# Attention logits of a graph network: one folded query weight, queries and keys on both partition halves, 64-row blocks that alternate between the halves

## The reference, cut to what matters

```python
h = jnp.maximum(_layernorm(x, axis=-1), 0.0)
x = x + _L1_gnn_ref(h, adj, W1, W2, W3, U1, U2, ln_g, ln_b)

# in _L1_gnn_ref
def _top_p_attention(X, W1, W2, W3):
    q = X @ W1.T @ W2.T            # W1 64 x 128, W2 64 x 64
    k = X @ W3.T                   # W3 64 x 128
    logits = q @ k.T / TAU         # 2048 x 2048, contraction 64
    probs = jax.nn.softmax(logits, axis=-1)
    idx = jnp.argsort(-probs, axis=-1)
    sp = jnp.take_along_axis(probs, idx, axis=-1)
    cs = jnp.cumsum(sp, axis=-1)
    keep_sorted = cs - sp < TOP_P
    ...
    A = probs * mask
    return A / jnp.maximum(A.sum(-1, keepdims=True), 1e-12)
for n in range(STEPS):             # 2
    A = _top_p_attention(Xa, W1, W2, W3)
    Xf = R @ Xf                    # R: adj + eye, rows normed
    Xa = A @ Xa
    Z = Z + Xf @ U1[n].T + Xa @ U2[n].T
```

## Time and profile before

| | us |
|---|---|
| median of 3 runs (lowest, highest) | 1067.96 (1066.7, 1069.11) |
| span of the profiled execution, first to last instruction | 1063.4 |
| TensorE busy, VectorE busy, ScalarE busy | 838.8, 779.5, 510.0 |
| mean granted clock of TensorE | 0.899 of 2.4 GHz |

### The profile page before, as it was taken

The page is one execution under the profiler, slowest core; times in us unless marked ns, Lnnn a source line. Parts: engine busy times, 40 slices in busy tenths (PEclk is TensorE's granted clock), DMA queues, the critical chain, the costliest instruction groups (busy, mean ns, idle before and its releaser), DMA issues.

```text
span 1063.4 us, 12286 instructions
## 1 busy us (share of the span) xinstructions
PE 838.8 (79%) x3886; PEld 566.1 (53%) x3886; DVE 779.5 (73%) x2363; ACT 510.0 (48%) x979; POOL 69.7 (7%) x68
## 2 busy tenths in 40 slices
PE   5889958887887853939779878868658999996695
PEld 4844425655665642737256557547447475553342
DVE  5968779888987998971697899889789702326715
ACT  4877235357368376413552664674775232023212
POOL 0020110000000000000000000010001100002201
PEclk9899998998988995969799789989789999998798
DMA  9849304424004000000043320230260456500001
GB/s 339 344 174 431 119 8 151 132 106 159 1 1 159 1 0 2 1 2 1 1 158 124 108 88 1 79 136 1 59 269 15 153 238 253 221 1 0 1 0 40
DMA packets 20221, 108.25 MB, mean 102 GB/s; under 512 B 1824, under 2 KB 8752, under 8 KB 9776
## 3 DMA queue, kind: packets, MB, share of 16 engines
q1 hardware_dynamic: 18752, 106.77, 27.0%
q10 hardware_dynamic: 1392, 0.61, 0.2%
HBM read 88.23 MB, written 19.14 MB: 101 GB/s over the span
## 4 chain that ended last, share of the span: by engine, by line
PE 46%; DVE 27%; ACT 13%; issue 9%; POOL 2%; DMA 1%; DVEq 1%; POOLq 0%; SPq 0%; ACTq 0%
PE PS L808 10%; DVE AT L1520 8%; PE PS L743 6%; PE PS L676 5%; PE PS L546 5%; DVE mxv L1659 4%; PE PS L877 3%; ACT BC L1249 3%; ACT AT L1249 3%; DVE nd L1523 3%; PE PS L1060 3%; PE PS L1036 3%; PE PS L1066 2%; DVE AT L2106 2%; ACT AT L1082 2%
## 5 line engine op out<-in xcount | busy, mean ns | idle before, releaser
L1082 ACT ACTIVATE AT<-PS 128x512 f32<-128x512 f32 (+2 forms) x240 | 118.8, 561 | 121.3 <-PE PS L546 103.7
L743 PE MATMUL PS<-K,ST 128*128 128x512 f32 x224 | 125.6, 713 | 13.0 <-ACT EA L1217 7.6
L546 PE MATMUL PS<-ident,AT 128*128 128x128 f32 x544 | 85.5, 293 | 55.4 <-DVE rS L2161 24.5
L1520 DVE SCALAR_TENSOR_TENSOR AT<-EA,se 128x2048 uint8<-128x2048 f32 (+1 forms) x46 | 107.6, 2345 | 1.6 <-DVE se L1513 0.3
L546 PEld LDWEIGHTS PS<-ident,AT 128*128 128x128 f32 x544 | 68.7, 152 | 64.0 <-DVE rS L2161 26.1
L1520 DVE SCALAR_TENSOR_TENSOR AT<-AT 128x2048 uint8<-128x2048 f32 (+2 forms) x48 | 96.1, 2002 | 2.0 <-PE PS L546 1.1
L1659 DVE TENSOR_REDUCE mxv<-PS 128x1 f32<-128x2048 f32 x32 | 73.3, 2289 | 26.0 <-PE PS L743 20.4
L743 PEld LDWEIGHTS PS<-K,ST 128*128 128x128 f32 x224 | 49.4, 232 | 73.1 <-issue 73.0
L2106 DVE MAX8 AT<-AT 128x8 f32<-128x256 f32 x256 | 87.6, 412 | 0.7
L808 PE MATMUL PS<-hr,AT 128*128 128x128 f32 x512 | 69.8, 285 | 9.2 <-ACT AT L1082 8.4
L808 PE MATMUL PS<-AT 128*128 128x128 f32 x512 | 68.3, 281 | 8.7 <-ACT AT L1082 8.1
(11 more groups left out here) (297 smaller groups left out, 1473.1 us busy)
## 6 DMA issues: line engine op xcount, KB each, us to landing
AT<-keep_at SPq DMA_DIRECT2D x32, 1024.0 KB, 5.1
EA<-in_adj SPq DMA_DIRECT2D x20, 1024.0 KB, 6.8
keep_at<-AT SPq DMA_DIRECT2D x8, 2048.0 KB, 24.9
AT<-keep_at SPq DMA_DIRECT2D x8, 2048.0 KB, 12.3
AT<-in_adj SPq DMA_DIRECT2D x12, 1024.0 KB, 5.0
EA<-keep_degrees SPq DMA_DIRECT2D x1, 1024.0 KB, 6.5
keep_x<-K SPq DMA_DIRECT2D x4, 256.0 KB, 8.6
out<-EA SPq DMA_DIRECT2D x4, 256.0 KB, 2.3
```

The costliest lines, as they stand in the source:

```text
L546: return pe.transpose(dst, src, ident[0:p, 0:p])
L743: mm = pe.matmul(bank(half(gi, k) + n), ST[1][:, k * P:(k + 1) * P], wide_keys[:, n * BK:(n + 1) * BK], start=True, stop=True)
L1082: return act.activation(dst, src, ACT.Copy)
L1520: return dve.scalar_tensor_tensor(out=o, in0=x0, scalar=s, in1=x1, op0=op0, op1=op1, **k)
```

## The change

The two query weights become one. After the weights are turned, TensorE multiplies `W1` (as loaded, 64 rows) with the turned `W2` into bank 3, and ScalarE copies the 128 x 64 result twice, side by side, into the slot `QT`, which takes the place of `W1T`; `W3T` is stored twice in the same way. A query or key call now has 128 columns of weights, and its result stands on partitions 0 to 63 and again on 64 to 127. The second query product, its copy, and the semaphores around them go. The first query moves out of `MEANWHILE` to where its second half stood. The zeroing by GpSimd and `zero_ok` go. Each logits call contracts 64 rows: the lower half of the partitions for even key blocks, the upper for odd ones. The mean contracts all 128, so its factor halves.

```diff
-W1T, W3T, W2T, U1T, U2T, L2WT, L3WT = 0, 1, 2, 3, 5, 7, 8
+QT, W3T, W2T, U1T, U2T, L2WT, L3WT = 0, 1, 2, 3, 5, 7, 8
-        keys = K[0:DA, :, :].rearrange("p t c -> p (t c)")
-        wide_keys = K[:, :, :].rearrange("p t c -> p (t c)")
+        keys = K[:, :, :].rearrange("p t c -> p (t c)")
...
-                pool.memset(K[DA:P, b * G:(b + 1) * G, :], 0.0).then_inc(zero_ok, 1)
...
-            pool.memset(ST[1][DA:P, :], 0.0).then_inc(zero_ok, 1)
...
             pe.wait_ge(wt_ok, 6)
+            pe.matmul(bank(3)[:, 0:DA], raw[0:DA, 0, :], WT[0:DA, W2T, 0:DA], start=True, stop=True).then_inc(qw_mm, 1)
...
-                pe.matmul(bank(n)[0:DA, :], WT[:, W3T, 0:DA], XT[:, n * BK:(n + 1) * BK],
-                          start=True, stop=True).then_inc(k_mm, 1)
+                pe.matmul(bank(n), WT[:, W3T, :], XT[:, n * BK:(n + 1) * BK], start=True, stop=True).then_inc(k_mm, 1)
             def first_query():
-                pe.matmul(bank(7)[0:DA, :], WT[:, W1T, 0:DA], XT[:, 0:BK], start=True, stop=True).then_inc(t1_mm, 1)
-            def second_query():
-                pe.wait_ge(t1_out, 1)
-                pe.matmul(bank(7)[0:DA, :], WT[0:DA, W2T, 0:DA], ST[0][0:DA, :], start=True, stop=True)\
-                  .then_inc(q_mm, 1)
+                pe.wait_ge(wt_ok, 8)
+                pe.matmul(bank(7), WT[:, QT, :], XT[:, 0:BK], start=True, stop=True).then_inc(q_mm, 1)
             MEANWHILE = {3: lambda: first_rows(2), 4: lambda: hr_turned(0), 5: lambda: hr_turned(1),
-                         7: lambda: keys_of(0), 8: lambda: keys_of(1), 9: first_query}
+                         7: lambda: keys_of(0), 8: lambda: keys_of(1)}
...
             def queries(step, g):
...
-                pe.matmul(bank(7)[0:DA, :], WT[:, W1T, 0:DA], src[:, g * BK:(g + 1) * BK], start=True, stop=True)\
-                  .then_inc(t1_mm, 1)
-                pe.wait_ge(t1_out, gi + 1)
-                pe.matmul(bank(7)[0:DA, :], WT[0:DA, W2T, 0:DA], ST[0][0:DA, :], start=True, stop=True)\
-                  .then_inc(q_mm, 1)
+                pe.matmul(bank(7), WT[:, QT, :], src[:, g * BK:(g + 1) * BK], start=True, stop=True).then_inc(q_mm, 1)
...
-            def logit_part(k, n):
-                return pe.matmul(bank(4 * k + n), ST[1][:, k * P:(k + 1) * P], wide_keys[:, n * BK:(n + 1) * BK],
-                                 start=True, stop=True)
+            def logit_part(to, k, n):
+                half_rows = slice(0, DA) if n % 2 == 0 else slice(DA, P)
+                return pe.matmul(bank(to + n), ST[1][half_rows, k * P:(k + 1) * P],
+                                 keys[half_rows, n * BK:(n + 1) * BK], start=True, stop=True)
...
                 for n in range(4):
-                    mm = pe.matmul(bank(half(gi, k) + n), ST[1][:, k * P:(k + 1) * P],
-                                   wide_keys[:, n * BK:(n + 1) * BK],
-                                   start=True, stop=True)
+                    mm = logit_part(half(gi, k), k, n)
...
-            copy(WT[:, 0, 0:DA], bank(4)[:, 0:DA]).then_inc(wt_ok, 1)
-            copy(WT[:, 1, 0:DA], bank(4)[:, P:P + DA]).then_inc(wt_ok, 1)
+            for h in range(2):
+                copy(WT[:, W3T, h * DA:(h + 1) * DA], bank(4)[:, P:P + DA]).then_inc(wt_ok, 1)
...
+            act.wait_ge(qw_mm, 1)
+            for h in range(2):
+                copy(WT[:, QT, h * DA:(h + 1) * DA], bank(3)[:, 0:DA]).then_inc(wt_ok, 1)
...
             def queries(step, g):
                 gi = NB * step + g
-                act.wait_ge(t1_mm, gi + 1)
-                copy(ST[0][0:DA, :], bank(7)[0:DA, :]).then_inc(t1_out, 1)
                 act.wait_ge(q_mm, gi + 1)
-                copy(ST[1][0:DA, :], bank(7)[0:DA, :]).then_inc(q_out, 1)
+                copy(ST[1][:, :], bank(7)).then_inc(q_out, 1)
...
-                ts(mean, PS[:, 6, MEANS + G * par:MEANS + G * par + G], 1.0 / N, ALU.mult).then_inc(mean_ok, 1)
+                ts(mean, PS[:, 6, MEANS + G * par:MEANS + G * par + G], 0.5 / N, ALU.mult).then_inc(mean_ok, 1)
```

More of the change, by code:

```diff
@@ L223, in rows @@
             return PS[:, b, :].rearrange("p (k c) -> p k c", c=P)
-        names = """in_x in_small ident_ok expo_ok wt_t wt_ok nat_sum nat_act at_t at_out pw_in pw_out h_ready h_t h_st
+        names = """in_x in_small ident_ok expo_ok wt_t wt_ok qw_mm nat_sum nat_act at_t at_out pw_in pw_out h_ready h_t h_st
             s_mm s_out nd_ok deg_t deg_s deg_d1 deg_d2 y_ok ps_mm ps_st ps_t ps_u ps_row ps_z z_dma
-            sums x1_ok late_in dve_steps act_steps pool_steps k_mm k_out t1_mm t1_out q_mm q_out
+            sums x1_ok late_in dve_steps act_steps pool_steps k_mm k_out q_mm q_out
             logits_ok negmax_ok exp_ok round_steps kept_ok e_turned e_copied ex_mm ex_ok
@@ L452, in _ @@
             n += 2
[L453 to L457, removed]
-                pool.memset(K[DA:P, b * G:(b + 1) * G, :], 0.0).then_inc(zero_ok, 1)
-            for b in range(NB - 1):
-                power(sm[:, 3, :], sm[:, 2, :], 0, G, n + 1 + b)
[L462 to L466, removed]
-            pool.memset(ST[1][DA:P, :], 0.0).then_inc(zero_ok, 1)
-            pool.wait_ge(zero_ok, NB)
-            power(sm[:, 3, :], sm[:, 2, :], 0, G, n + NB)
+            for b in range(NB):
+                power(sm[:, 3, :], sm[:, 2, :], 0, G, n + 1 + b)
             n += NB
-            pool.wait_ge(pw_out, n)
-            keys_zeroed(NB - 1, NB)
-            pool.wait_ge(zero_ok, NB + 1)
             power(esc[:, :], cs[:, :], 1, NT, n + 1)
@@ L577, in _ @@
             pe.wait_ge(at_out, 4 * NT + 4)
-            turn(bank(4)[:, 0:DA], raw[0:DA, 0, :])
             turn(bank(4)[:, P:P + DA], raw[0:DA, 1, :])
@@ L684, in _ @@
             first_rows(NB - 1)
-            second_query()
+            first_query()
             keys_of(2)
@@ L722, in means @@
                     mm = pe.matmul(bank(6)[:, MEANS + G * (gi % 2) + k:MEANS + G * (gi % 2) + k + 1],
-                                   ST[1][0:DA, k * P:(k + 1) * P], ksum[0:DA, :], start=True, stop=True)
+                                   ST[1][:, k * P:(k + 1) * P], ksum[:, :], start=True, stop=True)
                 mm.then_inc(mean_mm, 1)
-            def logit_part(k, n):
-                return pe.matmul(bank(4 * k + n), ST[1][:, k * P:(k + 1) * P], wide_keys[:, n * BK:(n + 1) * BK],
-                                 start=True, stop=True)
+            def logit_part(to, k, n):
+                half_rows = slice(0, DA) if n % 2 == 0 else slice(DA, P)
+                return pe.matmul(bank(to + n), ST[1][half_rows, k * P:(k + 1) * P],
+                                 keys[half_rows, n * BK:(n + 1) * BK], start=True, stop=True)
             def logits(step, g, k):
@@ L883, in later_keys @@
                 pe.wait_ge(exT_ok, G * (n + 1))
-                pe.matmul(bank(n)[0:DA, :], WT[:, W3T, 0:DA], xaT[:, n * BK:(n + 1) * BK],
-                          start=True, stop=True).then_inc(k_mm, 1)
+                pe.matmul(bank(n), WT[:, W3T, :], xaT[:, n * BK:(n + 1) * BK], start=True, stop=True).then_inc(k_mm, 1)
             for step in range(STEPS):
@@ L898, in _ @@
                     pe.wait_ge(k_out, 4)
[L899 to L900 removed]
+                    logit_part(0, 0, 3).then_inc(logits_ok, 1)
                     means(0, 0)
[L902 removed]
+                    logit_part(4, 1, 3)
                     pe.wait_ge(mean_ok, 1)
[L904 removed]
+                    logit_part(4, 1, 2).then_inc(logits_ok, 1)
                     for k in range(2, G):
@@ L1143, in keys_of @@
                 act.wait_ge(k_mm, 4 * step + n + 1)
-                act.activation(keys[:, n * BK:(n + 1) * BK], bank(n)[0:DA, :], ACT.Copy,
-                               accum_out=ksum4[0:DA, n:n + 1]).then_inc(k_out, 1)
+                act.activation(keys[:, n * BK:(n + 1) * BK], bank(n), ACT.Copy,
+                               accum_out=ksum4[:, n:n + 1]).then_inc(k_out, 1)
             act.wait_ge(deg_d1, 16)
```

28 lines of the change are left out of this document (11 added, 17 removed).

## The result

The changed kernel takes **1084.97 us** (1083.47 to 1088.74, 4 runs) against 1067.41 for the kernel before on the same chip: a ratio of 1.0165, 95% interval 1.0143 to 1.0188. It is slower by 17.6 us, where 17 less were forecast; the range, 1042 to 1072, doesn't hold it. The profiled execution took 1088.74, its span is 1087.0 us.

The account below looks back on a forecast made before the run. No single engine bounds it; the chain changes hands between TensorE, VectorE and ScalarE. Gains on VectorE's waits and the start sum to 21.2 us, less 4 for clock falls: 17, so 1068 - 17 = 1051 us, range 1042 to 1072.

Parts of the forecast that it names:

- A logits tile: TensorE's eight logits instructions take five slots plus two changes, 2.49 us instead of 3.43, 0.95 less.
- The query and the start: One query matmul and copy start the sums 1.75 us earlier; the kernel's start gains net 1.4.
- the first rival: Halves run without overlap, clock kept: tiles cost +5, the query gives -6; 1067 us, chance 0.18.
- What is given back: TensorE idles longer ahead of each exponential, so its clock falls: three falls on the path, 4 us.
- Where it lands: Gains placed on VectorE's waits in the groups of steps 0 and 1, with 1.4 at the start: 21.2 us.
- the 0.43: VectorE's wait in the group after step 1's start, expected to go: 0.4 us.
- the 1.95: VectorE's wait in step 1's second group for a tile at the low clock, of which 1.5 go.
- the 2.74: VectorE's wait in the second group of step 1, expected to be all covered.
- the 4.44: VectorE's wait in step 1's third group, of which two tiles' 1.9 and a little more goes.
- Four slots: Rival: all logits calls run in pairs, 0.43 less on some 12 tiles; 1046 us, chance 0.10.
- Half rows at half clock: Rival: no overlap and TensorE's clock falls to 1.2 GHz in logits tiles, 7.2 each; 1085 us, chance 0.20.
- The rest 0.02: Chance left for anything beyond five slots, four slots, no overlap with clock kept, and half clock.

Follow-up runs that it names:

- experiment 1: Changed kernel with the equal-value tests at a row's cut made strict, so the repair never runs; 1047.53 us.
- The fold alone: Kernel before with only the two query weights folded into one product, logits still over 128 rows; 1104.53 us.
- experiment 9: Kernel before with W2 times 1.5 and the key weight times 2/3, nothing else; 1097.08 us.
- 5: Changed kernel with the folded query weight times 1.5 and the key weight times 2/3; 1068.99 us.
- 6: Changed kernel with the folded query weight times 1.25 and the key weight times 0.8; 1061.32 us.
- 12: Changed kernel with the folded query weight times 1.125 and the key weight times 8/9; 1049.68 us.
- experiment 10: Changed kernel without the repair, plus two unread TensorE calls ahead of the last transposes before the first logits; 1046.35 us.
- 11: Changed kernel, repair in, folded query weight times 1.75, key weight times 4/7, plus two unread TensorE calls before the first logits; 1060.14 us.
- Experiment 2: Changed kernel without the repair, all logits calls on rows 0 to 63 instead of alternating halves; 1114.75 us.

## Why the prediction was wrong

The mechanism came out, its price nearly, and the sign not. Taking experiment 1 as the change without the accident, by the table's groups:

| stretch, up to `rS` of | forecast | experiment 1 against before |
|---|---|---|
| step 0, first group | -3.4 | +0.5 |
| second | -3.8 | -4.2 |
| third and fourth | -0.6 | +0.5 |
| step 1, first | -5.7 | -7.1 |
| second | -4.2 | -4.6 |
| third | -3.5 | -5.1 |
| fourth and the end | 0 | -0.3 |
| given back by the clock | +4 | in the lines above |
| sum | -17 | -20.2 |

- **A logits tile**, 2.49 us forecast, is 1.92 at the full clock. The mis-sized term is the number of slots: four, not five. "The two instructions of one call share rows and can't overlap each other" isn't tested, and doesn't matter: by the count of slots the two of the next call run in the other half at the same time. Two changes of shape cost 0.20 together, not 0.34. The Trainium skill (TensorE: Matmul & The Clock Gate, Part 3) says that calls on different rows run side by side; the four slots agree with it, though no single start is visible in these rows.
- **The query and the start.** The fold alone has its first row maximum at 137.42 instead of 139.11, 1.7 us sooner, where 1.4 was forecast. One execution can't confirm it: in experiment 9, with the instructions of the kernel before, it comes at 140.52. Ahead of the repairs it gains 6.8; the first rival's sum had 6.
- **What is given back** shows most at a place that I hadn't named, the start: 3.9 us worse than forecast, close to the 4 taken for three falls elsewhere. A single execution places it only roughly. The five traces with the same instructions up to there (the changed kernel, 1, 5, 6 and 12) have `rS` of the first group at 258.58 to 261.96, the two that are filled (10 and 11) at 257.62 and 255.52. Between the means lie 3.9 us, so the idle time is the cause of most of it.
- **Where it lands** held by groups: the first and second of step 1 and its third are 0.4 to 1.6 us better than forecast. By single waits it is rougher. In experiment 1 the 0.43 and the 1.95 of the earlier trace rows are gone; of the 2.74, which were to go wholly, 0.66 are left, and of the 4.44, of which some 2 were to go, 1.13.
- **The rivals.** Four slots, given 0.10 and 1046 us, is what the traces show: experiments 1 and 12 took 1047.5 and 1049.7. Half rows at half clock, given 0.20 and 1085 us, has the measured time, but not its reason: with alternating halves a tile takes 1.92 at the full clock and 3.72 where the granted clock is 0.50 (at 617.50 in the kernel after), and without the repair the kernel is 20 us faster than before. Experiment 2 shows that the rival was real for a kernel without overlap: its tile takes 7.09 at a granted clock of 0.50, as the 7.2 of the working.
- **The step that failed** stands in "How the numbers follow": "The rest 0.02". Every case there takes VectorE's list of instructions as given, and so puts what the change adds on VectorE at nothing. It isn't given: `group` holds branches on the data, and a change of rounding moves them. The runs showed two repairs in its place, 26 instructions that cost 37.4 us (1084.97 against 1047.53) where the change itself gains 20.4. That they came in this draw is bad luck, as 12 shows; that nothing in the prediction allowed for them is the error. The signs were in the trace of before. Its VectorE stands still for 6.32 us with "issue" as the only cause ahead of the last group's masks:

```profile
833.82 0.19 DVE L1759 TENSOR_REDUCE fl<-ft 128x1 int32<-128x32 int32 x1
840.33 2.35 DVE L1520 SCALAR_TENSOR_TENSOR AT<-AT,s 128x2048 f32<-128x2048 f32 x1 [6.32 <-issue]
```

In the code a flag is read and a branch decided between these two lines, in a kernel in which no group needs a repair. A case "the fold rounds differently, and some row tiles are repaired", at 14 to 37 us above 1051, would have put the slow side of the range where it belongs. From the profile alone its chance couldn't be had.

What stays open: whether the fold makes equal values more likely. With it, four of five sets of digits had a repair (5 row tiles), without it one of three (2 row tiles); that is too few to tell. All of them lie in the last two groups of step 1; why these is open too. A repair with fewer flag reads wasn't tried.

## What to carry to other kernels

Where a kernel branches on values, any change of rounding, even a weight product regrouped, is a change of the instruction stream: look for the branches, price both sides from rows, and compare two kernels with the branch disabled or over several meaningless scalings, since one draw measures luck. When a forecast mechanism is visible in the trace and the time goes the other way, find the last point at which the new kernel is still ahead; here one table of a single instruction's start times led to the cause. Two calls that contract 64 rows each belong on different halves, next to each other: on the same half a tile's four calls take eight slots instead of four.

## What the runs showed of the hardware that was not expected

- Calls in fp32, two instructions each, overlap fully when neighbours use different halves of the rows: 1.92 us for eight instructions against 3.63 on one half. On one half the granted clock is lower too, 0.839 on average against 0.876, and the kernel is 67 us slower (experiment 2).
- Skipping code can cost VectorE more than entering it. In the last group, the time from the flag to the first mask is 6.32 us where the branch is skipped (before) and 2.15 where it is entered, in the kernel after. All fourteen traces agree: 6.19 to 7.61 in the eight that skip it, 2.15 to 2.17 in the six that enter it. The kernel after:

```profile
840.41 0.19 DVE L1724 TENSOR_REDUCE fl<-ft 128x1 int32<-128x32 int32 x1
842.75 2.35 DVE L1485 SCALAR_TENSOR_TENSOR AT<-AT,s 128x2048 f32<-128x2048 f32 x1 [2.15 <-issue]
...
865.62 2.35 DVE L1485 SCALAR_TENSOR_TENSOR AT<-AT,s 128x2048 f32<-128x2048 f32 x1 [13.70 <-issue]
868.01 4.42 DVE L1991 TENSOR_TENSOR_SCAN AT<-AT 128x2048 f32<-128x2048 f32 x1
```

- Inside, the way to the one row tile that needs its scan costs 13.70 us, more than the 12.0 of the repair's own instructions. The Trainium skill (Runtime: NRT & Kernel Launch, Instruction fetch mechanics) says that a branch to code that isn't loaded yet waits for its transfer; 6.32 against 2.15 agrees. So do the queues that carry instructions; here one of them in the kernel before from 833.80 to 840.40, then in the kernel after from 851.90 to 865.70 (packets, MB, share):

```profile
q14 instruction: 1, 0.01, 0.3%
```

```profile
q14 instruction: 2, 0.02, 0.4%
```

Over all fourteen traces, from 240 us on and for gaps above 1.5 us, each of VectorE's 28 "issue" gaps of 4.64 to 7.61 us holds one packet of that queue, each of the 6 of 11.20 to 13.70 us two, and of the 93 of 1.72 to 2.36 us 89 hold none. So the long gaps go with transfers of instructions, and the short ones show what flag reads and branches take without one. No run here takes the transfer away, so that it is the cause is likely, not shown.
- 2.18 us of idling on TensorE, ahead of a chain of short steps, cost 2.4 us at the next row maximum (141.54 against 139.18), and two calls whose result nobody reads bring them back at that place (experiment 10). The five traces with that wait have a granted clock of 0.66 to 0.73 from 130 to 142 us, the two that are filled 0.96 and 0.98.
